# Windowed attention and a recurrent gate network: where a double slot's turns, values and scores stand in TensorE's order, and where ScalarE makes x2's high half

## The reference

```
x1 = x + attention(layernorm(x), ctx, ctx) @ W_proj.T + b_proj
     # 16 heads of 32; scores * 32**-0.5; keys further than 64 rows away are masked; softmax
x2 = layernorm(x1)
c  = in_c                                  # recurrent over the 8 batches
for b in range(8):
    f = sigmoid(x2[b] @ wf.T + c @ uf.T + bf)
    i = sigmoid(x2[b] @ wi.T + c @ ui.T + bi)
    g = tanh(x2[b] @ wc.T + c @ uc.T + bc)
    c = f * c + i * g
out = x1 + tanh(x2 @ wo.T + c @ uo.T + bo)
```

## Time and profile before

| | us |
|---|---|
| median of 3 runs | 938.56 (938.07 to 938.91) |
| profiled execution, its own time | 939.05 |
| its span, first to last instruction | 937.2 |
| TensorE busy | 920.3 (98%) |
| VectorE busy | 674.9 (72%) |
| ScalarE busy | 476.7 (51%) |
| GpSimd busy | 206.0 (22%) |

### The profile page before, as it was taken

One profiled execution on the slowest core, in us unless ns is written; L12 is line 12 of the kernel. 1 busy time (PEld: TensorE's weight loads), 2 busy tenths in 40 slices (PEclk: granted clock), 3 DMA queues, 4 the chain that ended last, 5 costly groups with the idle time before them and its releaser, 6 DMA issues.

```text
span 937.2 us, 21983 instructions
## 1 busy us (share of the span) xinstructions
PE 920.3 (98%) x7842; PEld 716.2 (76%) x7842; DVE 674.9 (72%) x2275; ACT 476.7 (51%) x1430; POOL 206.0 (22%) x236
## 2 busy tenths in 40 slices
PE   7999899999999999999999999999999999999998
PEld 5555567677887788878787888788877888888887
DVE  6888987888779977997799878987798531143222
ACT  6888666655555544555465555555555321131222
POOL 5576322211111111111111111111101100003444
PEclk9999999999999999999999999999999999999999
DMA  9564223224443443434543444344333150059862
GB/s 303 165 200 145 86 80 108 87 69 130 132 139 112 130 132 92 143 108 129 133 141 109 119 116 125 108 109 109 98 99 92 50 164 0 1 178 384 316 233 101
DMA packets 139348, 123.58 MB, mean 132 GB/s; under 512 B 46824, under 2 KB 104168, under 8 KB 137704
## 3 DMA queue, kind: packets, MB, share of 16 engines
q1 hardware_dynamic: 138520, 121.91, 42.9%
q10 hardware_dynamic: 720, 0.27, 0.2%
HBM read 87.70 MB, written 34.46 MB: 130 GB/s over the span
## 4 chain that ended last, share of the span: by engine, by line
PE 89%; DVE 5%; ACT 2%; issue 2%; DMA 1%; SPq 0%; DVEq 0%; ACTq 0%
PE ps_g L706 18%; PE ps_g L708 18%; PE ps_g L707 18%; PE ps_a L753 5%; PE ps_a L775 5%; PE ps_m L706 3%; PE ps_v L796 3%; PE ps_m L708 3%; PE ps_m L707 3%; PE ps_m L828 2%; PE ps_a L708 2%; PE ps_a L706 2%; PE ps_a L707 2%; ACT probs L923 2%; PE ps_v L801 2%
## 5 line engine op out<-in xcount | busy, mean ns | idle before, releaser
L923 ACT ACTIVATE probs<-probs,rowmin 128x192 f32<-128x192 f32 (+1 forms) x512 | 239.4, 470 | 114.0 <-DVE rowmin L1035 114.0
L1035 DVE CUSTOM_DVE_ANT_0 probs<-ps_a,mask 128x192 f32<-128x192 f32 (+1 forms) x512 | 166.1, 386 | 28.4 <-PE ps_a L753 26.8
L706 PE MATMUL ps_g<-state_hi,gate_w 128*128 128x512 f32 x336 | 133.6, 398 | 0.0
L708 PE MATMUL ps_g<-state_hi,gate_w 128*128 128x512 f32 x336 | 131.1, 390 | 0.0
L707 PE MATMUL ps_g<-state_lo,gate_w 128*128 128x512 f32 x336 | 130.8, 389 | 0.0
L1070 DVE STREAM_TRANSPOSE keys<-probs 32x128 f32<-32x128 f32 x420 | 125.5, 299 | 5.6 <-issue 0.2
L970 ACT ACTIVATE gate<-ps_g,bias 128x512 f32<-128x512 f32 x84 | 57.6, 686 | 105.8 <-PE ps_g L708 105.1
L923 ACT ACTIVATION_READ_ACCUMULATOR probs<-probs,rowmin 128x1 f32 x512 | 96.4, 188 | 0.0
L928 ACT ACTIVATE probs_t<-ps_a 128x512 f32<-128x512 f32 x108 | 59.3, 595 | 61.1 <-PE ps_a L775 61.1
L685 POOL TENSOR_TENSOR attn_lo<-recip,attn_hi 128x512 fp32r<-128x512 f32 x23 | 29.7, 1292 | 275.8 <-ACT attn_hi L936 275.8
L706 PE MATMUL ps_g<-x2t_even,gate_w 128*128 128x512 f32 x192 | 80.5, 419 | 0.0
(11 more groups left out here) (220 smaller groups left out, 1723.5 us busy)
## 6 DMA issues: line engine op xcount, KB each, us to landing
values<-ctx_rows SPq DMA_DIRECT2D x34, 256.0 KB, 4.4
xr<-x SPq DMA_DIRECT2D x32, 256.0 KB, 3.8
keys<-ctx_t SPq DMA_DIRECT2D x16, 512.0 KB, 4.2
x_dram<-xr SPq DMA_DIRECT2D x32, 256.0 KB, 2.6
gate_w<-x2t_dram SPq DMA_DIRECT2D x8, 1024.0 KB, 10.1
keys<-ctx_t SPq DMA_DIRECT2D x16, 384.0 KB, 3.4
x2t_dram<-x2t_even SPq DMA_DIRECT2D x12, 512.0 KB, 4.4
x2t_dram<-x2t_odd SPq DMA_DIRECT2D x12, 512.0 KB, 4.5
```

The source lines that it names most:

```text
L706: pe.matmul(ps, lhs[0], rhs[0], start=start, stop=False)
L708: return pe.matmul(ps, lhs[1], rhs[0], start=False, stop=stop)
L923: act.activation(row, row, ACT.Exp, bias=rowmin[:, i % 2, h:h + 1], scale=-1.0, accum_out=rowsum[:, i // G % 2, i % G, h:h + 1]).then_inc( ...
L1035: dve.tensor_tensor_reduce(probs[:, i % 2, h, 0:SEEN[t]], ps_a[h][:, score_at[i]:score_at[i] + SEEN[t]], mask[:, MASK0[t]:MASK0[t] + SEEN[ ...
```

## The change

In double slots TensorE's list becomes: turn of n, values of n-2 and n-1, turn of n+1, scores of n+2 and n+3, and then the cells, with the projection behind five of them. Odd turns go to `ps_m`, so that the scores need only wait for ScalarE's copy of turn n. Further, in the lists of the other engines: the masks are a step of their own (`mask`) behind the sides of this double slot, which were one double slot earlier; mult and halves of a tile are done in the first double slot of the next tile; ln1 and the reciprocals come later; turn2_hi of the second double slot stands behind the copies of the turns. The waits are set anew to fit.

```diff
@@ in the list of steps, n >= FIRST_TWO
-            steps.extend(("turn", m) for m in both)
-            if s == 0:
-                tile_steps("ln1", i + 2)
+            back = [m for m in (n - 2, n - 1) if FIRST_TWO <= m < SLOTS]
+            steps.extend(("turn", m) for m in both[:1])
+            steps.extend(("value", m) for m in back)
+            steps.extend(("turn", m) for m in both[1:])
+            steps.extend(("score", m) for m in ahead)
+            if s == 0 and i - 1 >= SENT:
+                tile_steps("mult", i - 1)
+                tile_steps("halves", i - 1)
+            if s == 2 and i - 2 in MOVED and i - 1 in MOVED:
+                tile_steps("turn2_hi", i - 2)
+            late_sides = [m for m in both if m >= FIRST_TWO + 2]
+            steps.extend(("sides", m) for m in late_sides[:1])
             cells(2)
...
             gates(2)
-            steps.extend(("score", m) for m in ahead[:1])
+            steps.extend(("sides", m) for m in late_sides[1:])
             if s == 2 and i - 1 not in MOVED:
                 tile_steps("turn2_lo", i - 1)
-            steps.extend(("score", m) for m in ahead[1:])
+            steps.extend(("mask", m) for m in ahead)
...
             steps.extend(("exp", m) for m in ahead)
-            steps.extend(("value", m) for m in both)
-            if s == 0:
-                tile_steps("proj", i - 1)
-            else:
-                tile_steps("mult", i)
             gates()
             renew()
             cells(3)
-            steps.extend(("recip", m) for m in ahead[:1])
             if s == 0:
+                tile_steps("proj", i - 1)
+            gates()
+            if s == 0:
+                tile_steps("ln1", i + 2)
+                steps.extend(("recip", m) for m in ahead)
                 tile_steps("resid", i - 1)
                 tile_steps("stat2", i - 1)
-            else:
-                tile_steps("halves", i)
-            steps.extend(("recip", m) for m in ahead[1:])
-            if s == 0:
                 tile_steps("send", i)
-            steps.extend(("sides", m) for m in ahead[:1])
             if s == 0 and i + 1 >= TURNED_X:
                 tile_steps("query_norm", i + 1)
+            if s == 0 and i - 2 in MOVED:
+                tile_steps("turn2", i - 2)
+                if i - 1 not in MOVED:
+                    tile_steps("turn2_hi", i - 2)
+            gates()
+            cells(7)
...
             gates(3)
-            steps.extend(("sides", m) for m in ahead[1:])
+            if s == 2:
+                steps.extend(("recip", m) for m in ahead)
             renew()
@@ banks and waits
-        ps_turn = [ps_g[0] if n < OWN_BANKS else ps_a[n % 2 if n >= FIRST_TWO else 0] for n in range(SLOTS)]
+        ps_turn = [ps_g[0] if n < OWN_BANKS else ps_m if n >= FIRST_TWO and n % 2 else ps_a[0] for n in range(SLOTS)]
...  score on TensorE
-                        pe.wait_ge(turned_a, i - i % 2)
+                        pe.wait_ge(turned_a, i - i % 2 - 1)
...  turn on TensorE, odd slots
+                            pe.wait_ge(recip_out, SENT)
+                            pe.wait_ge(x1_done, tile - 1 + (i % G) // 2)
+                            pe.wait_ge(x2_lo, split_by(tile - 1))
+                            pe.wait_ge(q_ready, min(tile + 1 + (i % G) // 2, TURNED_X))
...  proj and turn2 on TensorE
+                            pe.wait_ge(turned_a, min(G * (i + 1) + 2, SLOTS))
+                        pe.wait_ge(turned_a, min(G * (i + 1) + 4, SLOTS))
...  the copy of a turn on ScalarE, and likewise sides on VectorE
-                    need(act, valued, i - i % 2 if i >= FIRST_TWO else i)
+                    need(act, valued, i - 1 if i >= FIRST_TWO + 2 else i - i % 2 if i >= FIRST_TWO else i)
```

More of the change, by code:

```diff
@@ L215, in bass_xattn_ffn @@
                 tile_steps("query_out", i + 1)
[L216 to L220, removed]
             if s == 0 and i - 1 not in MOVED:
@@ L769, in _ @@
                     if i >= FIRST_TWO:
+                        tile = i // G
                         pe.wait_ge(masked, HPG * (i - i % 2 + 2))
+                        if i % 2:
+                            pe.wait_ge(recip_out, SENT)
+                            pe.wait_ge(x1_done, tile - 1 + (i % G) // 2)
+                            pe.wait_ge(x2_lo, split_by(tile - 1))
+                            pe.wait_ge(q_ready, min(tile + 1 + (i % G) // 2, TURNED_X))
                     else:
@@ L841, in _ @@
                     need(pe, column_turned, len([n for n in row_at if n < G * (i + 1) + 2]))
+                    if i + 1 >= SENT:
+                        pe.wait_ge(turned_a, min(G * (i + 1) + 4, SLOTS))
                     for k in range(G):
@@ L1027, in _ @@
                     dve.tensor_tensor(queries[:, :, :], queries[:, :, :], rstd, ALU.mult).then_inc(q_ready, 1)
-                if kind == "score":
+                if kind == ("mask" if isinstance(i, int) and i >= FIRST_TWO + 2 else "score"):
                     t = i // G % TT
@@ L1059, in _ @@
                     dve.wait_ge(expd, HPG * (i + 1))
-                    dve.wait_ge(valued, i - i % 2 if i >= FIRST_TWO else i)
+                    dve.wait_ge(valued, i - 1 if i >= FIRST_TWO + 2 else i - i % 2 if i >= FIRST_TWO else i)
                     if i == OWN_BANKS:
```

## The result

The changed kernel takes 946.36 us (945.92 to 946.91, 4 runs) against 938.32 for the one before: ratio 1.0086, 95% interval 1.0069 to 1.0103. It is 8.0 us slower. The forecast was 947.5, in a range of 935 to 957.

A forecast was written before the change was run, and what follows sets the result against it. TensorE's own order of work was taken as the bound (89% of the span). Crossings +6.2 and boundary waits +2.7 sum to +8.9 on the profiled 939.05: 947.9, as a median 947.5; 8-in-10 range 935 to 957.

The forecast's parts named there:

- The crossings: TensorE's double slots: two more changes between the 128*128 and small forms cost +0.13 a slot, 6.2 us in all.
- The scores' wait for the copy: TensorE's scores need ScalarE's copy of turn n: there at 1.85, scores reached at 2.12, so no cost.
- The batch boundary: First scores wait for VectorE's late queries once in eight slots: five boundaries at 0.55, +2.7 us.
- VectorE takes over: Rival, chance 0.18: GpSimd's additions stretch blends, middle tiles run late and TensorE waits for VectorE: 958, range 952 to 962.
- nothing less to do: VectorE's order: the change takes no work from VectorE and gives it new idle time.
- One visit is what counts: Rival, chance 0.17: TensorE pays for entering attention work, not for each form; faster, 930, range 928 to 937.
- The ends: First double slot without its values, last values a visit of their own, tail the same: together about 0.
- turn2_hi: x2's high half on ScalarE, moved behind the copies: TensorE never waited for it, so the gain is nothing.

The follow-up runs named there:

- b_cell_between: Kernel before, with one cell (three matmuls) moved between a double slot's scores and its values, two crossings more: 949.46 us, ratio 1.0114.
- b_turns_apart: Kernel before, with one cell moved between the two turns of a double slot, no crossing more: 938.83 us against 938.91, ratio 0.9999.
- a_cells_cover: Changed kernel with turn, turn, value, value, two cells, score, score, still four crossings: 948.19 us, ratio 1.0101.
- a_turns_together: Changed kernel with both turns first, then values, then scores, two crossings in place of four: 961.40 us, ratio 1.0240.
- a_query_loaded_first: Changed kernel with query_norm ahead of the residual and stat2, and the queries' load ahead of keys and values: 943.87 us, ratio 1.0058.
- b_hi_behind: Kernel before, with x2's high half on ScalarE moved behind the copies of the next turns, nothing else: 938.60 us, ratio 0.9999.
- a_hi_ahead: Changed kernel with x2's high half back at its old place, ahead of the gate and the copies: 951.30 us, ratio 1.0138.
- a_query_first: Changed kernel with query_norm on VectorE ahead of the residual and stat2 instead of behind send: 952.62 us, ratio 1.0164.

## Why the prediction was right

*The crossings.* Predicted 3.11 for turns, values, scores and what cells lose, against 2.98: +0.13 a slot. Measured 3.11 in the middle tile shown above (0.52, 1.01, 0.59, 0.84, and 0.15 that the cells lose) and +0.15 a slot as a mean: second turns behind the values of edge tiles take 0.61, and in most second double slots of a tile the cells lose 0.17 to 0.20. The term is 6.6 where I had 6.2. b_cell_between shows that crossings alone cost such an amount and more, b_turns_apart that changes within the 128*128 form cost nothing. One price for every pair, though, was more than the rows gave: a_cells_cover and b_cell_between pay 0.22 to 0.23 where this order pays 0.15, which came out right because rows 4, like this change, have transposes between the small forms.

*The scores' wait for the copy.* Predicted none, with 0.3 of cover. Right: in the slot shown above ScalarE's copy ends at 510.27 and the scores start at 510.50, behind the second turns without a gap.

```profile
509.67 0.60 ACT L942 ACTIVATE probs_t<-ps_a 128x512 f32<-128x512 f32 x1 [0.60 <-PE ps_v L812]
```

The cover is really 0.1, by the 0.14 that a_turns_together shows from a copy's end to the scores.

*The batch boundary.* Predicted 0.55 for five boundaries, found 0.3. The chain was right and each term a little long: in the slot from 482.98 mult started at +3.03 (3.4), masks ended at +10.98 (11.2), queries were ready at +16.13 (16.6), and the slot was 13.83 long (14.0). So queries came at 2.3 of the next slot and the scores started at 2.40. VectorE's rows of that stretch, first the blend, state halves and mult, then the queries:

```profile
482.74 0.69 DVE L1170 SCALAR_TENSOR_TENSOR gate<-gate,state 128x512 f32<-128x512 f32 x1 [2.35 <-ACT gate L984]
483.46 0.69 DVE L1173 SCALAR_TENSOR_TENSOR state<-gate 128x512 f32<-128x512 f32 x1
...
484.22 1.86 DVE L1184 SCALAR_TENSOR_TENSOR state_lo<-state,state_hi 128x512 fp32r<-128x512 f32 x3
486.01 0.68 DVE L1094 TENSOR_TENSOR recip<-ps_v,recip 128x512 f32<-128x512 f32 x1
```

```profile
497.72 0.66 DVE L1039 TENSOR_TENSOR queries<-queries,tile_row 128x512 f32<-128x512 f32 x1
498.42 0.69 DVE L1041 TENSOR_TENSOR queries<-queries,tile_row 128x512 f32<-128x512 f32 x1
```

The idle 2.35 ahead of the blend is the idle time that sides filled before. The size of this term is mis-set by 1.2 us in all, 2.7 against 1.5, and I missed the one wait of 0.28 for a copy; that the wait is real and is the queries' is shown by the row at 499.21 and by a_query_loaded_first.

*VectorE takes over,* the rival at 958: not seen. It hung on blends stretched by GpSimd's addition. Both steps take 0.69 here, where one took 1.65; in the new order the addition runs from 498.76 to 500.24, beside the sides, which take 1.88 for six as before. Of the 23 us by which VectorE's busy time fell, 20 are these two steps (58.9 us before, 38.8 after), against my "nothing less to do", and it brought no gain that can be seen, since TensorE was hardly ever waiting for VectorE. GpSimd got longer instead: its step for stat2 takes 28.7 us in all and not 17.5, the addition 1.48 and not 1.29. That agrees with the Trainium skill's rule of the port that VectorE and GpSimd lock ("SBUF — State Buffer", section SBUF: two separate sides): which step is stretched is a matter of when the other engine runs.

*One visit is what counts,* the faster rival at 930: refuted: the changed kernel has the one visit and is slower, and a_cells_cover and b_cell_between show the crossings' price.

*The ends.* I had them at about 0; they gave 1.0 back. The values of the first double slot had 0.72 of waits and crossing around them where I had counted 0.51. The cells there lose 0.15 and not 0.91, of which 0.25 was a wait of its own (L731 for VectorE's L1085); this I had not looked at. The turns take 0.50 longer, 0.24 of it the new wait of the scores, which I had at 0.4.

*turn2_hi.* Predicted worth nothing; in the order before it is (b_hi_behind). In the new order it isn't free to choose: a_hi_ahead costs 4.9 us by the medians. My sentence "the gain is nothing" holds against the kernel before only.

*The sum.* The two profiled executions differ by 7.5, where I had 8.9: order 6.6 (6.2), waits 1.8 (2.7), the wait that is gone -0.6 (not seen), ends -1.0 (0), and 0.7 that isn't of the change. The mechanism, crossings and the queries' wait, is what the runs show; that the total is only 1.1 us off is in part luck, since the misses have both signs.

## What to carry to other kernels

When TensorE is the bound, count how often its order goes from one tiling form to another, not how many pieces the order has: here 0.15 to 0.23 us for a pair of crossings, the more where 128x512 matmuls stand between the small forms, while transposes and 128x512 matmuls mix for next to nothing. Price the crossing from places in the trace where the same pairs of instructions already meet. Before an instruction is moved ahead on an in-order engine, look up when its slowest input lands, DMA issue order included: what stands behind it waits for that as well.

## What the runs showed of the hardware that I had not expected

- From the end of ScalarE's copy to the first score that waits for it pass 0.14 us behind values (507.49 to 507.63, a_turns_together) and 0.15 behind turns (526.59 to 526.74, a_hi_ahead). So the way from 128*128 into the scores' form adds next to nothing on top of such a wait.
- In a_query_first a load issued at 465.39, with keys and values just ahead, was waited for until 470.87, 5.5 us later; four issues of small blocks held SyncE's queue for 4.91 us.
- The same crossing doesn't always cost the same: turns behind an edge tile's values take 0.61 against 0.59, and the cells lose 0.15 in first double slots but 0.17 to 0.20 in most second ones. Why stays open, as does why cells between small forms cost more than a turn there.
